# Layer 1's causal attention: two heads stacked in 64-row f32r tiles, heads taken in quads, four diagonal blocks in one slot, values over two key blocks

## What is computed

```python
q = split_heads(x @ Wq + bq); k = split_heads(x @ Wk + bk); v = split_heads(x @ Wv + bv)   # 16 heads of 16
attn = jnp.einsum('bhqd,bhkd->bhqk', q, k) / jnp.sqrt(jnp.float32(D))
attn = attn + slopes[:, None, None] * (jnp.arange(T) - (T - 1))[None, None, :]
attn = jnp.where(causal, attn, jnp.finfo(jnp.float32).min)
p = jax.nn.softmax(attn, axis=-1)
o = jnp.einsum('bhqk,bhkd->bhqd', p, v).transpose(0, 2, 1, 3).reshape(B, T, C)
return o @ Wo + bo
```

## Time and profile before

| | us |
|---|---|
| median of 3 runs (lowest, highest) | 1563.48 (1560.52, 1567.82) |
| the profiled execution, its time | 1566.81 |
| its span in the profile | 1565.0 |
| PE busy | 1426.5 (91%) |
| DVE busy | 926.7 (59%) |
| ACT busy | 747.3 (48%) |
| POOL busy | 548.9 (35%) |
| mean granted clock of PE | 0.952 |

### The profile page before, as it was taken

The page is one execution under the profiler, slowest core; times in us unless marked ns, Lnnn a source line. Parts: engine busy times, 40 slices in busy tenths (PEclk is TensorE's granted clock), DMA queues, the critical chain, the costliest instruction groups (busy, mean ns, idle before and its releaser), DMA issues. The chain is left out here.

```text
span 1565.0 us, 20565 instructions
## 1 busy us (share of the span) xinstructions
PE 1426.5 (91%) x7287; PEld 841.9 (54%) x7350; DVE 926.7 (59%) x1719; ACT 747.3 (48%) x1368; POOL 548.9 (35%) x454
## 2 busy tenths in 40 slices
PE   6889999899999999999999968899579999879998
PEld 3533333355455555454545546788434444468887
DVE  5588776456666666666666344444458787544445
ACT  3457776654545454545453324233235555435553
POOL 4260162155565655656566522233200000101210
PEclk9979999999999999999999968899789999959999
DMA  7980000000000000000001011110076000101110
GB/s 292 179 114 1 2 21 7 1 1 0 1 1 0 1 1 1 1 1 1 1 1 42 0 41 39 36 55 27 1 168 93 1 1 1 50 21 41 41 41 27
DMA packets 20442, 53.04 MB, mean 34 GB/s; under 512 B 4630, under 2 KB 7464, under 8 KB 19123
## 3 DMA queue, kind: packets, MB, share of 16 engines
q1 hardware_dynamic: 20341, 51.73, 13.6%
HBM read 42.28 MB, written 8.39 MB: 32 GB/s over the span
## 5 line engine op out<-in xcount | busy, mean ns | idle before, releaser
L1631 POOL TENSOR_TENSOR Ps<-Ps,Pb 128x512 f32<-128x512 f32 x192 | 245.3, 1291 | 161.4 <-ACT Pb L1614 161.4
L1614 ACT ACTIVATE Pb<-bank 128x512 f32<-128x512 f32 x256 | 152.9, 597 | 287.5 <-PE bank L1603 235.0
L1575 DVE TENSOR_REDUCE mp<-bank 128x1 f32<-128x512 f32 x256 | 171.7, 687 | 141.6 <-PE bank L1568 139.7
L1062 DVE TENSOR_REDUCE mp<-bank 128x2 f32<-128x1024 f32 x128 | 153.6, 1222 | 48.4 <-PE bank L1054 48.0
L1121 ACT ACTIVATE Pb<-bank 128x512 f32<-128x512 f32 x256 | 133.2, 600 | 39.7 <-PE bank L1104 39.3
L1568 PE MATMUL bank<-qk1h,qk0h 128*128 128x512 f32 x256 | 135.7, 541 | 7.7 <-DVE mp L1575 7.7
L1600 PE MATMUL bank<-qk0h,qk1h 128*128 128x512 f32 x256 | 124.3, 486 | 6.1 <-DVE mrow L996 6.1
L1645 PE MATMUL bank<-Pb,kvx 128*64 128x512 f32 x512 | 124.0, 605 | 1.0 <-ACT Pb L1614 0.7
L1246 ACT ACTIVATE Pb<-bank 128x512 f32<-128x512 f32 x192 | 84.7, 489 | 80.2 <-PE bank L1233 57.4
L1214 DVE TENSOR_REDUCE mp<-bank 128x1 f32<-128x512 f32 (+1 forms) x192 | 97.8, 552 | 17.6 <-PE bank L1204 11.5
L1602 PE MATMUL bank<-qk0h,qk1l 128*128 128x512 f32 x256 | 101.2, 396 | 0.0
(11 more groups left out here) (341 smaller groups left out, 3265.5 us busy)
## 6 DMA issues: line engine op xcount, KB each, us to landing
wr<-wf SPq DMA_DIRECT2D x25, 256.0 KB, 2.6
wraw<-wf SPq DMA_DIRECT2D x8, 768.0 KB, 4.1
scratch<-stgr SPq DMA_DIRECT2D x4, 1024.0 KB, 3.9
scratch<-stg SPq DMA_DIRECT2D x4, 768.0 KB, 7.0
owT<-owT SPq DMA_DIRECT2D x1, 2048.0 KB, 9.9
qbn<-qbn SPq DMA_DIRECT2D x1, 1536.0 KB, 14.9
qstr<-scratch SPq DMA_DIRECT2D x12, 128.0 KB
kstr<-scratch SPq DMA_DIRECT2D x12, 128.0 KB
```

What stands on the lines that cost most here:

```text
L1062: e.tensor_reduce(mp[:, w % 3, :, j, kh], wide[slot][:], AX, ALU.max).then_inc(ring_ok, 1)
L1575: e.tensor_reduce(mp[:, u % 3, hd, j, kh:kh + 1], bank[b][:, 0:c], AX, ALU.max).then_inc(mp_ok[2], 1)
L1614: e.activation(Pbm[n % NPBM][:], bank[b][:], ACT.Exp, scale=SC0).then_inc(exp_ok[2], 1)
L1631: e.tensor_tensor(Ps[z][:], first, Pbm[n % NPBM][:], ALU.add).then_inc(sum_ok, 1)
```

## The change

- Layer 1's q and k are split into two f32r parts instead of three bf16 parts, and stacked as in layer 0: a pair of heads on rows 0 to 63 and 64 to 127 of `qst2` and `kst2`. Head pair hp holds heads 2hp and 2hp+1.
- A unit is now four heads (a quad) and one half of the queries, eight units. `pair_half` puts the first query half of **all** quads first (units 0 to 3), then the second half of all (4 to 7). A number w counts pairs and halves: w 0 to 7 are pairs 0 to 7 on the first half.
- Only the q and k blocks of heads 0 to 7 are projected ahead of the stage. Those of heads 8 to 15 are four steps among the first maxima ("project").
- Row maxima: the four diagonal blocks of a pair and half go into one slot of 4x128 columns per head, masked by two bf16 matmuls over 512 columns; what is left of the diagonal is j*128 columns for j of 1 to 3; for the second half, 512 columns more per j. So 96 reductions instead of 192.
- Scores: two matmuls per step on 64 rows each, and on the diagonal two mask matmuls of 128 rows behind them. 96 steps.
- Values: every second key block, eight matmuls, over both key blocks. Evacuation as in layer 0, 8 times instead of 32.
- The shift rows are set by POOL with memsets, 16 rows and then 2 rows each, and the three bias rows of k are loaded by POOL (`bias_ok`).
- SP: the extra rows (`qrow`, `krow0`, `krow1`) are no longer loaded by it; the stacks are 12 transfers per group, of f32 rows.

```diff
 def causal_order():
-    def at_step(u, k):
-        return [("clear",)] if (u, k) == (0, 0) else []
-    return attention_order(32, 1, True, 4, 2, (2, 2, 0, 2), lambda u: [], at_step, lambda u: [(0, [("evac", u)])])
+    lead, steps = 14, [(2 * u, pr, kt) for u in range(8) for kt in range(pair_keys(1, 2 * u)) for pr in range(2)]
+    maxima = [("max", w, j, kh) for w in range(16) for j, kh in pair_max(1, w)]
+    beside = [("project", b, h) for b in (2, 3) for h in range(2)]
...
+    for n in range(lead):
+        one_max()
+        if n % 2 and beside:
+            order.append(beside.pop(0))
+        done += 1
+    for s, (w, pr, kt) in enumerate(steps):
+        order.append(("st", w // 2, pr, kt))
...
+        while maxima and done < lead + s + 1 + min(s, 32) // 4:
+            one_max()
+            done += 1
...
+        if pr == 1 and kt % 2:
+            behind.append((s + 3, ("pv", w // 2, kt)))
+            if kt == pair_keys(1, w) - 1:
+                behind.append((s + 6, ("evac", w // 2)))
...
+    def pool_stack2(e, l, hps):
...
+            r, top = (slice(64 * par + 32, 64 * par + 32 + rows) for rows in (16, 2))
+            for st, value in ((qst2, 1.0 * l), (kst2, 1.0 - l)):
+                e.memset(st[r, hps, :].bitcast(F32), value).then_inc(ones2, 1)
...
+                if l:
+                    e.memset(st[top, hps, :].bitcast(F32), 1.0 - value).then_inc(ones2, 1)
...
+        if l:
+            for par in range(2):
+                e.dma_start(kst2[64 * par + 34:64 * par + 37, hps, :],
+                            a["krow"][par, :, hps, :].bitcast(F32R)).then_inc(bias_ok[hps.start // 4], 16)
...
     def pe_maxp(e, l, s):
...
         if (j, kh) == (0, 0):
-            e.wait_ge(stacked[min(hp // 2, 2)], STACKED2)
-            e.wait_ge(ones2, 4 if hp < 4 else 8)
+            e.wait_ge(stacked[min(hp // 2, 2)], STACKED * (l + 1))
+            e.wait_ge(ones2, (4 if hp < 4 else 8) if l == 0 else 8 + (8 if hp < 4 else 16))
+            if l:
+                e.wait_ge(bias_ok[hp // 4], 32)
...
+        if len(parts) > 1:
+            for a in range(2):
+                last = e.matmul(wide[slot][:, a, :].rearrange("p (j c) -> p j c", j=4), idb[:],
+                                maskq[:].unsqueeze(1).to_broadcast([128, 4, 128]), start=False, stop=True,
+                                skip_group_check=True)
...
     def pe_stp(e, l, s):
...
+        for a in range(2 if on_diagonal else 0):
+            b = TILEP[l][u, pr, kt, a][1]
+            e.matmul(bank[b][:, 0:128], idb[:], maskk[:], start=False, stop=True, skip_group_check=True).then_inc(st_mm[0], 1)
...
     def sync(e):
...
-        sp_scratch(e, 1, 0)
-        sp_scratch(e, 1, 1)
-        sp_stack(e, 1, 0)
-        sp_scratch(e, 1, 2)
-        sp_scratch(e, 1, 3)
-        sp_stack(e, 1, 1)
-        sp_stack(e, 1, 2)
+        sp_scratch2(e, 1, 0)
+        sp_scratch2(e, 1, 1)
+        sp_stack2(e, 1, 0)
+        sp_stack2(e, 1, 1)
+        sp_scratch2(e, 1, 2)
+        sp_scratch2(e, 1, 3)
+        sp_stack2(e, 1, 2)
```

More of the change, by code:

```diff
@@ L37, in numbered, with max_steps, attention_order @@
     return number
[L40 to L55, removed]
+def max_steps():
+    return [(a, j, kh, 512) for a in range(2) for j in range(4) for kh in range(2)]
+def attention_order(lag, at_begin, at_step, evac):
+    order, due, n, nu, nh, nk = [], [], 0, 16, 2, 2 * NT
     def steps_of(u):
-        return [("max", u, *s) for s in max_steps(nh, u % 2, causal)]
+        return [("max", u, *s) for s in max_steps()]
     def run_due():
@@ L90, in attention_order @@
             given += due_now
[L91 to L94, removed]
+            for _ in range(due_now // 2):
+                order.append(todo.pop(0))
+                due_now -= 1
             order.append(("st", u, a, kt))
@@ L1102, in pe_stp @@
             e.wait_ge(*free)
             r = slice(64 * a, 64 * a + 64)
[L1104 to L1109 removed]
+            last = e.matmul(bank[b][:, 0:c], kst2[r, hp, kt * 128:kt * 128 + 128], qst2[r, hp, q0:q0 + c],
+                            start=True, stop=True)
+            if not on_diagonal:
+                last.then_inc(st_mm[0], 1)
@@ new lines, in pe_pvp @@
+                e.wait_ge(vx_one, 2 * l + 1)
+                e.wait_ge(v_ok, 8 * l + NT)
+        n = TILEP[l][u, 1, kt, 1][0]
+        e.wait_ge(exp_ok[0], n + 1)
+        for t in kts:
+            c = tile_queries(l, half, t)[1]
+            for a in range(4):
+                hp = pair_half(l, 2 * u + a // 2)[0]
+                h, i = 2 * hp + a % 2, TILEP[l][u, a // 2, t, a % 2][0] - TILE0[l]
+                last = e.matmul(bank[6][32 * a:32 * a + 17, 512 - c:512], vx[:, t, h * 17:h * 17 + 17],
+                                PBR[l][i % len(PBR[l])][:, 0:c],
+                                start=(t == 0), stop=(t == pair_keys(l, 2 * u) - 1), skip_group_check=True)
@@ L1271, in act_ot16 @@
-    def act_ot16(e, s):
-        _, u, ready = s
-        half = u % 2
-        if ready[-1][1] != 4 * half + 3:
-            return
-        e.wait_ge(pv_mm[1], PV_MM0[1] + NO_C[s])
-        if u >= 2:
-            e.wait_ge(ev_mm[1], u - 1)
-        e.activation(OTa[half][:], bank[4 + half][:], ACT.Copy).then_inc(ot_ok[1], 1)
-    def pe_evac16(e, u):
-        half = u % 2
-        e.wait_ge(ot_ok[1], OT_OK0[1] + u + 1)
-        e.wait_ge(b6_ok[1], B6C["evac", u])
-        for j in range(4):
-            rows = 32 * (j + 1) if half == 0 else 128
-            last = e.matmul(bank[6][:, 128 + 17 * j:145 + 17 * j], OTa[half][0:rows, 128 * j:128 * j + 128],
-                            esum[0:rows, :], start=True, stop=True)
-        last.then_inc(ev_mm[1], 1)
@@ L2461, in tensor @@
         e.wait_ge(a0_ok, 64)
-        for blk in range(4):
+        for blk in range(2):
             for half in range(2):
@@ L2553, in vector @@
         dve_hn(e, 2, 1)
-        for blk in range(4):
+        for blk in range(2):
             for half in range(2):
-                dve_project(e, 1, blk, half)
+                dve_project2(e, 1, blk, half)
         for i in range(NT):
```

737 lines of the change are left out of this document (322 added, 415 removed).

## The result

The median of the changed kernel is 1641.8 us (1636.14 to 1650.68, 4 runs), that of the kernel before, beside it, 1565.1 (1560.52 to 1567.82, 4 runs). The ratio is 1.0498, 95% interval [1.0443, 1.0553]: 5% slower, +77 us. The forecast was +19.5 us and a range to 1601. The sign was right and the size was not. The profiled execution is the shortest of the four.

The account below looks back on a forecast made before the run. PE's instructions were taken to bound the stage: first maximum +1.2 us, lead and stall to 1218, then 155 us, ending at 1373 against 1353.5. That +19.5 on 1563.5 gave 1583 us, 8-in-10 range 1550 to 1601.

Parts of the forecast that it names:

- What bounds the kernel: Changed stage, 1164 to 1354: PE's list of instructions bounds it, busy 176.9 of 190.0 us, and ACT waits for it.
- the stall: PE, DVE and ACT idle some 21 us, from about 1197 to 1218, until the third stack group lands.
- Step 1: First maximum waits for POOL's memsets, to 1162.3, and a 3 us bias transfer: 1165.3, +1.2 us.
- Step 2: First maximum to last projection's remainder: 22 us, to 1187.3, with 3.4 for two casts waiting on POOL's memsets.
- Step 3: Third stack group (heads 8 to 15) lands 31 us after the last remainder, at 1218; PE waits some 21 us.
- Step 4: Work left after 1218: 93 score steps, 80 maxima, all values; 155 us, the end at 1373.
- Half clock after the stall: 4: Term for PE at half clock behind the wait for the third stack group: 4 us of the 155.
- Worse on both sides: Rival, slower, chance 0.12: casts wait whole memsets, landing at 1224, masks 0.5, 168 us left: +39, 1602.
- Columns decide: Rival, faster, chance 0.17: narrow steps cost by columns, masks hide in ACT waits; 105 + 4 us left, -26, 1537.
- ACT's pace: Rival, no change, chance 0.20: masks near 0.12, PE has slack, ACT needs 127 + 4 us; -4, about 1559.
- The drain at each change of the tiling mode: At each mask, a pair's whole modelled tail lost, 0.25 more: 15 us worse, not taken into the forecast.
- The 512 matmuls of maxima, scores and masks: Prediction's count for maxima and scores with their masks, of which two heads now go in the time of one.

Follow-up runs that it names:

- e5: Changed kernel with kst rows filled first and the bias transfer issued behind four memsets instead of eight; 1625.2 us.
- e1: Changed kernel with both query halves of a quad in sequence and 16 maxima ahead instead of 14; 1613.0 us.
- e2: Changed kernel with values over one key block at a time, twice as many visits of half the length; 1608.1 us.
- e3: Changed kernel without mask matmuls on scores and maxima, so not causal inside diagonal blocks; 1614.5 us.
- e16: Changed kernel with each layer 1 score pair computed twice, first over all 512 queries and never read; 1633.2 us.
- e13: e12 with one maximum per score step and the last ones spread, so 12 end steps have none, not 26; 1567.1 us.
- e14: e13's instructions reordered: first query half first, 12 maxima ahead, the rest only as needed; 1607.8 us.
- e12: e7 with each quad's second 512 queries first and the cast of negated maxima written as a tensor_tensor; 1577.1 us.
- e6: Changed kernel with the edits of e1 and e2 together; 1600.1 us.
- e7: e6 with e5's edit and all four projections of q and k ahead of the values; 1581.8 us.
- e4: Changed kernel with diagonal score matmuls over all 512 queries of their half, mask and exp as before; 1638.7 us.
- e11: e7 with diagonal score matmuls over all 512 queries, as in e4; 1581.5 us.

## Why the prediction was wrong

- **What bounds the kernel**: right for what is left behind the stall, where PE is busy for 182.7 of 195.1 us. Before the first scores it also waits for transfers and for DVE.
- **Step 1**, first maximum +1.2 us: the memsets were right, the transfer's 3 us were 14.3 (12.6 from issue to landing), and outside its bounds of 0 to 4. The rows behind these bounds show the gap ahead of a transfer on SP, not one that has to land beside full engines. e5 shows it: with the bias out of the way the maximum comes 11.3 us sooner. +11.4 us against the forecast.
- **Step 2**, 22 us to the last remainder: 19.2 measured (1174.03 to 1193.21). The casts did not wait in this run, since the first (1182.55) came in the last 0.1 us of a memset and the second (1192.17) after the last one. That was luck of timing: in e1 and e2 a cast at the same place takes 3.39 and 3.55 us, and PE then waits 4.6 and 4.8, so step 2 had the mechanism right. -3 us.
- **Step 3**, landing 31 us after: 33 (1193.2 to 1226.25), and the stall 20.1 for 21. Right, and the stall costs its length, as e1 shows (stage 21.7 us shorter).
- **Step 4** is the step that failed: "Half clock after the stall: 4". It took the earlier trace rows, a clock of 0.54 and 0.50 for 8 us after the pause and then 1.00, as a property of any stage. From 1226 to the end the clock is 0.78, so 86 us at half: 43 us, not 4. The sum of the other terms holds, 195.1 less 43 is 152, for 151 without the 4, but not each of them: by e3 all masks cost about 24 us and not 35, so the rest costs some 10 more than step 4 has, and in which term is open. So that the sum fits is in part luck. e2 and e16 show that the clock is the cause. What takes it is open.
- The terms for -3, +11.4, +2 and +40 make 50.5, and with the forecast's 19.5 the 70 us of the two executions.
- **Rivals**: "Worse on both sides" had the right side and 1602; of its reasons only the late landing came true (1229 in the time of the kernel before, for 1224). "Columns decide" has 109 us behind the stall and "ACT's pace" 131; measured are 152 even at full clock, and 130 without any masks (e3), so both were wrong without the clock. No rival had half clock. That the form takes work from PE is right: e13's full-clock length is 164 against 184 before, and 62 us at half clock give 31 of it back.
- **The drain at each change of the tiling mode** (the Trainium skill, TensorEngine Tiling (Array Packing), "Key Properties"), 15 us more by the prediction's estimate: e3's 24 us for all masks leave no room for it beside 35 without it.
- The 512 matmuls of maxima, scores and masks are 640 in the kernel before (192, 192 and two times 128); no term of the sum uses the number.

## What to carry to other kernels

An edit that takes work from TensorE can cost it its clock: price the stage at both clocks, and look at the granted clock of stretches that have the new mix of work. A busy share of 95% says nothing about it; instructions of the engine behind it per stretch do. The order alone can decide: e13 and e14 have the same instructions, and 41 us lie between them. Spreading the maxima over the stage helped here (e12 to e13, 10 us), but no run tells beforehand which order holds the clock. And a small transfer that a first instruction waits for is issued before the large ones fill the engines.

## What was not expected of the hardware

- TensorE at half clock with 20.00 of 20 us busy and no wait (e14), and a kernel that does not get slower with 192 more matmuls (e16). Which kind of work holds the clock is open: the same values work in visits of 8 instead of 16, with maxima between them, stood at 1.00 from 1240 to 1358 (e2), but e6, e7 and e14, with such visits too, fell to half again and again; wider or doubled score pairs came with less half clock (e4, e11, e16).
- A bias transfer (48 KB) took 12.6 us to land beside full DMA engines, 7.4 in e5, which issues it 13.5 us earlier, and 2.7 for the second group of the changed kernel, issued at 1190.
- A memset of 2 rows costs what one of 16 rows does, 3.50 us for 4096 columns.
- An 8-column cast on VectorE waits until GpSimd's memset ends, 3.07 us; the same written as a tensor_tensor takes 0.17.
